# A new order for the pieces of five images in one round of a software-pipelined pass

## Time and profile before

| | |
|---|---|
| median of 3 runs | 1477.58 us (1475.88 to 1477.93) |
| profiled execution | 1476.25 us, of which the span from first to last instruction is 1474.5 us |
| PE busy | 976.5 us (66% of the span) |
| DVE busy | 763.3 us (52%) |
| ACT busy | 597.5 us (41%) |
| POOL busy | 401.3 us (27%) |
| mean granted clock of TensorE | 0.76 |

### The profile page before, as it was taken

How to read it: one execution, slowest core, us unless ns; L and a number is a source line. 1 busy time by engine, 2 the same in 40 slices (tenths; PEclk the granted TensorE clock), 3 DMA queues, 4 the chain that set the end, 5 groups by cost and what they waited for, 6 DMA issues and landing times.

```text
span 1474.5 us, 26072 instructions
## 1 busy us (share of the span) xinstructions
PE 976.5 (66%) x8998; PEld 671.1 (46%) x8998; DVE 763.3 (52%) x2165; ACT 597.5 (41%) x1259; POOL 401.3 (27%) x525
## 2 busy tenths in 40 slices
PE   0266667666564434677777877767777878767876
PEld 0154555554343233354464563554544645534454
DVE  1156666555342444476465564564754655645342
ACT  0255556555351011433444425334334444254542
POOL 3377777776001021211111212111111112111000
PEclk9987676767585555787786886887877878878776
DMA  3000000000000100000000000000000000000000
GB/s 96 9 10 11 10 9 11 9 9 7 6 0 16 26 24 22 24 13 22 23 6 25 15 19 25 15 19 25 9 21 25 8 25 15 19 23 4 4 3 3
DMA packets 51853, 24.46 MB, mean 17 GB/s; under 512 B 37977, under 2 KB 49802, under 8 KB 51818
## 3 DMA queue, kind: packets, MB, share of 16 engines
q1 hardware_dynamic: 51818, 24.01, 6.5%
HBM read 16.10 MB, written 7.88 MB: 16 GB/s over the span
## 4 chain that ended last, share of the span: by engine, by line
PE 24%; issue 18%; DVE 11%; ACT 9%; POOL 3%; DMA 1%; DVEq 0%; SPq 0%; ACTq 0%; POOLq 0%
PE ps L1240 20%; ACT stackt L1042 3%; DVE nm L920 3%; DVE xs L899 2%; DVE samp L896 2%; ACT prob L1198 1%; PE ps L1245 1%; ACT L1198 1%; POOL srstd L516 1%; POOL hatr L592 1%; PE ps L1543 1%; DVE th L880 1%; DVE hat L881 1%; ACT th L1152 0%; ACT hb L1224 0%
## 5 line engine op out<-in xcount | busy, mean ns | idle before, releaser
L1042 ACT COPY stackt<-ps 128x768 bf16<-128x768 bf16 x192 | 142.8, 829 | 92.2 <-PE ps L1245 92.1
L1240 PE MATMUL ps<-stackt 53*64 53x64 bf16 (+3 forms) x2304 | 111.3, 247 | 87.5 <-ACT stackt L1042 50.6
L1240 PE MATMUL ps<-b_xnt,we 128*128 128x256 f32 x384 | 143.5, 494 | 2.6 <-ACT hb L1224 2.3
L1224 ACT ACTIVATE hb<-ps 128x512 f32<-128x512 f32 (+1 forms) x128 | 63.1, 493 | 202.3 <-PE ps L1240 202.1
L552 POOL TENSOR_TENSOR rn<-ss,neghalf 128x24 f32<-128x24 f32 x32 | 132.7, 4163 | 42.1 <-DVE ss L749 42.1
L920 DVE TENSOR_REDUCE nm<-ps 128x2 f32<-128x512 f32 x192 | 120.5, 685 | 30.1 <-PE ps L1240 26.9
L1198 ACT ACTIVATE prob<-ps 128x512 f32<-128x512 f32 x192 | 104.2, 594 | 63.9 <-PE ps L1240 63.8
L1240 PEld LDWEIGHTS ps<-stackt 53*64 53x64 bf16 (+3 forms) x2304 | 49.1, 115 | 170.8 <-issue 58.8
L516 POOL TENSOR_TENSOR prstd<-pveps,neghalf 128x2 f32<-128x2 f32 x48 | 42.5, 885 | 309.8 <-DVE pveps L709 302.5
L1240 PEld LDWEIGHTS ps<-we,hb 128*128 128x128 f32 x768 | 110.7, 220 | 26.0 <-ACT hb L1224 20.5
L1240 PE MATMUL ps<-we,hb 128*128 128x96 f32 x768 | 111.8, 303 | 15.8 <-ACT hb L1224 15.8
(11 more groups left out here) (229 smaller groups left out, 1676.4 us busy)
## 6 DMA issues: line engine op xcount, KB each, us to landing
rows<-xn_scratch SPq DMA_DIRECT2D x96, 48.0 KB, 1.9
hatst<-hat_scratch SPq DMA_DIRECT2D x96, 48.0 KB, 2.1
xn_scratch<-xnp SPq DMA_DIRECT2D x48, 48.0 KB, 1.8
hat_scratch<-hatp SPq DMA_DIRECT2D x16, 144.0 KB, 1.9
xraw<-x_scratch SPq DMA_DIRECT2D x16, 96.0 KB, 2.0
out<-acc SPq DMA_DIRECT2D x16, 96.0 KB, 1.8
we<-in_we SPq DMA_DIRECT2D x1, 768.0 KB
xin<-in_x SPq DMA_DIRECT2D x16, 48.0 KB, 1.8
```

The source lines that it names most:

```text
L1042: return a.copy(stackt[:, x, :, P * t:P * t + P], bank_bf(bank))
L1224: a.activation(hb[:, e % 2].rearrange("p m n -> p (m n)")[:, 2 * TOK * k:2 * TOK * k + n_], ps[:, 6, 0:n_], ACT.Gelu).then_inc(S("c_h"), 1)
L1240: return m.matmul(o, l, r, start=start, stop=stop)
```

## The change

The string `ORDER_C` is replaced. It has the same letters in the same numbers (16 e, 16 a, 13 o, 8 s, 3 k); `BEHIND_C` and every piece stay as they are.

```diff
-ORDER_C = "eeeoeeosaeaasaseeeoaaeeeaooseoeaokokkeaeassaasooaaoasoao"
+ORDER_C = "eeaoeeaeaoeaeeoaeaosaeeeooeaeokekoasseosaasaosaaaoooskas"
```

## The result

| | before | after |
|---|---|---|
| median | 1477.32 us (4 runs) | 1289.89 us (1284.62 to 1294.98, 4 runs) |
| ratio to before | | 0.873, 95% interval 0.869 to 0.877 |
| profiled span | 1474.5 us | 1289.9 us |

The prediction was 1361 us with a range of 1325 to 1412.

What follows compares the result with a forecast made beforehand. Latency was taken as the bound: chains hopping between engines, and in-order queues where ready pieces stand behind waiting ones. Savings of 89 (full rounds), 10 (filling) and 17 (emptying), 116 us, took 1477.6 to 1361 us, range 1325 to 1412.

Steps and rivals of the forecast that it cites:

- Term 1: Behind the projection: a0's transposes and copies fit PE's idle 2.98 us; cost nil, 2.8 us if the cover were gone.
- Term 2: In A: s0, s1, s2 leave VectorE's list ahead of `f_xn`; 20.9 us becomes 15.2, bounds 14 and 17.
- A: Part of a full round from the projection's end to the transpose of `f_xn`, VectorE's list; 20.9 us, forecast 15.2.
- Term 3: In B: PE's new list takes 12.0 us plus 2.0 for half clock; 14.0 against 13.2, bounds 10.8 and 17.5.
- B: Part of a full round from the transpose of `f_xn` to a7's transposes; 13.2 us, forecast 14.0.
- Term 4: In C: 4.9 us to first exp, exps 11.3, tail 5.2; 21.4 us, bounds 19 and 24.2.
- C: Part of a full round from a7's transposes to the next projection's end; 23.5 us, forecast 21.4.
- Terms 5 and 6: Filling rounds save 10 us, bounds 0 and 15; emptying rounds save 17 us, bounds 8 and 22.
- No rival: Four rivals: clock takes half, about 1410 us (0.17); C serialised, 1443 (0.07); slower, 1588 (0.03); nothing changes, 1477 (0.03).
- the second: Rival in C: each exp step waits for the sampling piece ahead in PE's queue; about 1443 us, chance 0.07.
- e13: Piece of pass C's order, on PE in B; its move behind a7 was counted as 1.6 us less in B.

Runs made afterwards that it cites:

- b_a0: The kernel before with only a0 moved, from behind s0 to behind e1; 1468.09 us, ratio 0.9945.
- a_a0back: The kernel after with only a0 moved back, from behind e1 to behind e3; 1367.49 us, ratio 0.9281.
- a_searly: The kernel after with sampling pieces s0, s1 and s2 moved back ahead of o2; 1400.69 us, ratio 0.9487.
- a_back_mm: a_a0back with 24 matmuls of the identity added behind e1, into a bank nobody reads; 1347.24 us, ratio 0.9031.
- b_cspread: The kernel before with only the heaps between the exp steps dissolved (o8, s5, o9, s6 moved); 1417.76 us, ratio 0.9602.
- a_cheap: The kernel after with s4 and s5 together behind a9, o8 and o9 together behind a11; 1377.70 us, ratio 0.9337.
- b_mm: The kernel before with 24 identity matmuls added behind the projection, nothing moved; 1465.81 us, ratio 0.9924.
- b_three: The kernel before with three moves together: a0 behind e1, sampling pieces late, exp heaps dissolved; 1372.03 us, ratio 0.9315.

## Why the prediction was too slow

**Term 1, a0 into the gap: cost nil, as said.** The transposes took 1.50 us and ended before `b_xn`; the transpose of `b_xn` waited 0.26 us. Its gain "later" had no number of its own. b_a0 puts it at 8 us from before. Taking a0 out of the gap again costs 78 us from after, but in a_a0back it goes to another place, right ahead of a1, so the two are not one move measured twice.

**Term 2, A: 15.2 forecast, 14.0 measured.** The three sampling pieces are worth at least 5.5 us by a_searly, where 5.2 stood. The rest fits the gate at full clock, which had been named as a bound (14) and not taken: A is 14.0 where the half clock begins 5.6 us or more behind the projection, and 14.9 in the round where it begins after 4.2.

**Term 3, B: the step that failed most, 14.0 against 11.0.** Of this, 2.0 was the half-clock stretch that I expected "at B's start", from a gap of about 3 us ahead of `f_xn`. That is what one round in twelve does, the one at 916: a gap of 2.86 us, 3.41 us of half clock in B, B 12.56, which is 1.6 more. (In the second profiled execution it is also one round, with B at 15.25.) In the others PE's half-clock stretch fell into A, where PE had time, and stretched its work until `f_xn` was ready: the wait ahead of `f_xn` was at most 0.73 us. So the mechanism exists, and the step that failed is that the sum charged it to every round. That B takes 14.04 us in the slow rounds of a_back_mm, the very number forecast, is chance: it is 10.98 and 3.06 there, and was 12.0 and 2.0 in the sum. The other 1.0 is that PE's pieces overlap: the count by difference, 10.8, was nearer than the sum of durations, 12.3, and I took a value between them.

**Term 4, C: 21.4 against 19.3.** First to last exp took 9.7 us, where I took 11.3. The fear that the sampling pieces hold up the exps was right for pieces in a heap (b_cspread, a_cheap) and wrong for one piece per step: with a single piece between steps, PE waited for `samp` once a round. The tail grew by 0.1, not 0.7. The prediction had 8.9 as the lower bound of this stretch and gave it too little weight. It also started from 14.1, a time with PE at half clock for most of it (952.71 to 959.53 among others), and had no term for the clock in C. Before has 10.2 to 13.7 us of half clock in C in every round, and after has none.

**Terms 5 and 6.** Filling gave 15.3 us counted from C's first piece, 10 forecast and 15 the bound. Emptying gave 11.1, and 15.1 in the second profiled execution, 17 forecast.

**The sum.** The rounds missed by 6.1 us (1.2 in A, 3.0 in B, 2.1 in C for the round shown; the mean round is 0.2 longer), 73 us in twelve. Half of it or more is one wrong assumption: that the shorter round keeps as much half clock on PE's path. The sum kept the gate at half clock in A, added 2.0 for it in B, and took times measured at half clock in C. The runs show half clock off the path in ten rounds of twelve. The rest is sizes: 1.0 for PE's overlap in B, 0.6 for a tail that hardly grew, and a part of C's 1.6 that is not separated from the clock's. No rival came. The wait that the second was made of, for `samp`, is seen in a_cheap, where pieces stand together, and hardly where one stands between two steps.

**The clock.** The earlier trace rows had 20.4 us of PE's work at half clock in a round. What the change removed of that shows as PE's busy time, 77 us less in the loop. The 11 us of b_mm are no measure of what the clock can give in the old order, as most of its rounds kept the half clock in C; those that lost it in part were 1.6 to 2.8 us shorter between first and last exp. The clock's share in the 187 us can't be told apart cleanly: it acts only where PE is on the path, and the moves change both.

The Trainium skill's rule that transposes do not count as busy PE ("TensorE: Matmul & The Clock Gate", Part 4: PE-mode transpose) is not what these runs show. With 24 transposes in the gap the loop's mean clock was 0.90, with 24 matmuls 0.89, and with neither 0.84. By time the two are alike as well, 0.9056 and 0.9031 with intervals that overlap. The measurement decides, for bf16 transposes of 128 x 128 among other matmuls.

## What is left open

b_three and after differ by 82 us, 5.9 us a round: 1.9 in A, 1.9 in B and 2.3 between first and last exp, less 0.2 elsewhere. Undoing the maxima's alternation in after costs 1.5, nearly all in A, and undoing the place of q 3.2, nearly all in B. Neither touches the exps, so their 2.3 us belong to moves that were not tried alone: s6 out of the exps to the end of the round, with s7, k2, o11 and o12, the places of s4, s5 and o9, and e13 behind a7. Undone one by one from after, five moves cost 6.5 + 8.5 + 7.0 + 1.5 + 3.2 = 26.7 us a round, twice the 13.5 that all gave. What decides in which rounds the half clock falls into A and in which into B is open, and so is the difference of up to 38 us between executions of a_back_mm.

## What to carry to other kernels

In a pipeline of in-order queues, look for two pieces of one chain that stand next to each other on an engine: the second can wait out a round trip (0.79 us for s5 behind s4, 0.46 for o9 behind o8), and everything behind it waits too. Put one independent piece between them; dissolving two such heaps was worth 59 us by itself, with the clock that came back. And judge a move in the order it will live in: five moves taken back one at a time from after cost 26.7 us a round in sum, where all moves together had given 13.5.

## What was unexpected of the hardware

- Added work can make the kernel faster: 24 matmuls, 1.50 us in all, in an idle gap of sixteen rounds took 23 us (all executions) to 37 us (those that count for the ratio) off a_a0back, with a mean clock of 0.89 instead of 0.84 in the loop of the profiled one.
- Half clock can repair itself: rounds of a_back_mm take 51.1 or 48.8 us with the same instructions. Where the half-clock stretch falls into a part that waits for VectorE it is free, and the next part then runs at full clock.
- VectorE's product L871 takes 0.95 to 0.96 us beside GpSimd's splitting (L533), and 0.36 us in the early filling rounds without it. No run took the splitting away from it, so that this is the cause is not shown.
